# Cross-attention and expert layer: the router and the query sums moved behind two up blocks, the order at both ends rebuilt

## Chip, cores and metric

The kernel runs on one core of one Trainium2 chip. The metric is the device time of one execution, in microseconds (us). TensorE does the matrix products, VectorE is called DVE, ScalarE ACT, GpSimd POOL, SyncE SP.

## What is computed

There are 32 batches of 256 rows of width 256, a context of 77 rows for each batch, and a mask over these 77 rows. The layer normalization of the rows gives queries, keys and values; the context is normalized with learned vectors and gives further keys and values, so that each of the 256 queries sees 333 keys in 4 heads of 64. Queries and keys are normalized to unit mean square. Behind the attention stands a second layer normalization and a layer of experts: a router takes two of eight experts for each row, from the better of two groups, and a shared block is added.

```python
def attention(x, latents, mask):          # x: context, latents: normalized rows
    xn = layernorm(x, ln_x_g, ln_x_b); ln = layernorm(latents, ln_l_g, ln_l_b)
    q = ln @ W_q
    kv = concatenate([xn @ W_kv, ln @ W_kv], axis=1)
    sim = einsum('bhid,bhjd->bhij', rmsnorm(q, q_gamma) * SCALE, rmsnorm(k, k_gamma))
    attn = softmax(where(full_mask, sim, -max))
    return einsum('bhij,bhjd->bhid', attn, v) @ W_out + b_out
...
topk_idx, topk_w = _route(x, gate_weight, gate_bias)   # sigmoid, best group of 2, two experts
r2 = maximum(einsum('th,eih->tei', x, up_weights), 0) ** 2
routed = einsum('tei,ehi,te->th', r2, down_weights, cw)
sh = maximum(x @ shared_up_weight.T, 0.0)
shared = sh * sh @ shared_down_weight.T
...
x = x + attention(ctx, _layernorm(x), mask)
x = x + experts(_layernorm(x))
```

## The kernel before

Each 32-bit product is made of three: every operand is split into a rounded high part and the low part that is left, and `split_product` (lines 292 to 297) adds high by high, high by low and low by high. So beside each product stand small operations that make the low parts: `hid_lo`, `x_lo`, `q_lo`, `k_lo`, `at_lo`, `ln_lo`, and for the weights `w_lo`, `up_lo`, `down_lo`.

The batches run in a pipeline of steps. Step b does the attention of batch b, the experts of batch b - 1, and the first layer normalization and the projections of batch b + 1. The first step has no experts, the last no projections, and a tail behind it does the experts of the last batch. Each engine has a program of its own whose order is written out by hand in its `step` function (TensorE from line 520, ScalarE from 731, DVE from 1079, GpSimd from 1271); semaphores order the engines among each other, and an engine that waits holds back all that stands behind in its program.

TensorE's step begins with `transpose_k` (the keys, line 362). Then come `sum_q_squares` (line 349: 32 small products, 32 columns at a time, that sum the squares of each query) and `router` (line 465: 32 more of that kind). Then two of the six up blocks of the experts, two pairs of score blocks (lines 383 to 387), two up blocks, two pairs of score blocks, the shared down block, and then the transposes of the probabilities between the first down blocks and the last up blocks. The second half has the product with the values (line 411), the projections, the down blocks 2 to 7 and `transpose_x2` (line 452), which brings the twice normalized rows into place for the next router.

PSUM is shared out as four banks for attention (`attn_ps`), two for up (`up_ps`) and two for down (`down_ps`). The sums and the router's logits are written to `attn_ps`, the down blocks alternate between the two banks of `down_ps`, and DVE adds each of them to `acc` (`add`, line 1067), weighted with `route_w`.

DVE's step: `k_low`, the statistics of the next batch, four masked score blocks with their row maxima (`mask_scores`, line 906), `negate_max` (line 913, which needs the scales of the queries), the first eight levels of the routing (lines 996 to 1017), four more masked blocks, and then the rest of the routing between the adds of the experts. GpSimd's step: `q_scales`, the low parts of the hidden pairs 0 to 2 (`low`, line 1268), `rstd_first`, `residual` (`x_res`, line 1242), the low parts 3 and 4, `ln_low`, the low part 5 and the powers for the next batch. `q_scales`, `k_scales` and both `rstd` are powers with the exponent -1/2 (line 1223); the others are sums and differences of two tensors. Ahead of the steps DVE and ScalarE split the weights in parts; the low parts of the up weights (`up_parts`) stand in DVE's first step, those of the down weights in GpSimd's first step (line 1282).

## Time and profile before

| what | before |
|---|---|
| median of 3 runs | 1172.76 us (1172.66 to 1172.81) |
| the profiled execution | 1171.52 us |
| its span | 1169.7 us |
| busy TensorE | 1145.7 us, 98% of the span |
| busy DVE | 1006.4 us, 86% |
| busy ACT | 801.6 us, 69% |
| busy POOL | 555.2 us, 47% |

The span runs from the first to the last instruction of the profiled execution; the rest of its time lies around it. A row of an engine's instructions in order of time gives the start in us from the begin of the span, the length in us, the engine, the line of the kernel, the operation with its result and operands, and how many alike are grouped; in brackets stands the idle time before it, with what ended that. Where the bracket is missing, the engine had no idle time before the row. Lengths of TensorE's instructions overlap, so the distance from one start to the next is what counts. A clock of 1.00 is TensorE's full clock, 0.50 half of it.

### The profile page before, as it was taken

The numbers are of one execution on the slowest core, as the hardware profiler recorded it, in microseconds if no ns is written. First come the engines' busy times: TensorE is split into PE (matmuls) and PEld (weight loads), VectorE is DVE, ScalarE is ACT, GpSimd is POOL, SyncE is SP. The second block draws the span as 40 slices with busy tenths as digits, with TensorE's granted clock in tenths as the row PEclk, the third lists the DMA queues.
The fourth block names the chain that finished last, engine by engine and source line by source line (L and its number), as shares of the span: only waits on it lengthen the run. The fifth ranks groups of instructions, "written<-read, shape, count | busy, mean of one in ns | idle before, by whom it ended". The sixth has DMA issues, their size and how long they took to land. (4 is left out here: it accounts for less than half of the span.)

```text
span 1169.7 us, 32985 instructions
## 1 busy us (share of the span) xinstructions
PE 1145.7 (98%) x11772; PEld 1070.1 (91%) x11772; DVE 1006.4 (86%) x3500; ACT 801.6 (69%) x1900; POOL 555.2 (47%) x473
## 2 busy tenths in 40 slices
PE   7799999999999999999999999999999999999997
PEld 6699999999999999999999999999999999999997
DVE  6688988889888889888899888899888899888877
ACT  5577766677766768766778666678666677666673
POOL 5445444445444445454445454444454444454442
PEclk8899999999999999999999999999999999999999
DMA  5000000000000000000000000000000000000000
GB/s 173 13 14 23 23 22 12 14 23 23 23 12 22 14 23 22 23 11 23 14 22 23 23 11 22 13 23 23 22 11 22 14 23 22 23 10 15 10 11 19
DMA packets 28145, 26.06 MB, mean 22 GB/s; under 512 B 6544, under 2 KB 27440, under 8 KB 27984
## 3 DMA queue, kind: packets, MB, share of 16 engines
q1 hardware_dynamic: 27904, 23.83, 6.5%
q8 instruction: 95, 1.56, 0.6%
q14 instruction: 66, 0.54, 0.2%
q0 software_dynamic: 80, 0.14, 0.1%
HBM read 15.57 MB, written 8.39 MB: 20 GB/s over the span
## 5 line engine op out<-in xcount | busy, mean ns | idle before, releaser
L1268 POOL TENSOR_TENSOR hid_lo<-relu,hid_hi 128x512 fp32r<-128x512 f32 x192 | 248.3, 1293 | 246.6 <-DVE hid_hi L1052 166.2
L295 PE MATMUL down_ps<-down_hi,hid_hi 128*128 128x256 f32 x768 | 233.6, 304 | 1.7 <-ACT hid_hi L726 1.0
L1067 DVE SCALAR_TENSOR_TENSOR acc<-down_ps,route_w,acc 128x256 f32<-128x256 f32 x512 | 222.0, 475 | 8.9 <-PE down_ps L297 8.2
L295 PE MATMUL up_ps<-x_hi,up_hi 128*128 128x256 f32 x768 | 226.8, 295 | 0.0
L297 PE MATMUL down_ps<-down_hi,hid_lo 128*128 128x256 f32 x768 | 215.9, 281 | 0.0
L296 PE MATMUL down_ps<-down_lo,hid_hi 128*128 128x256 f32 x768 | 215.7, 281 | 0.0
L296 PE MATMUL up_ps<-x_lo,up_hi 128*128 128x256 f32 x768 | 214.3, 279 | 0.0
L297 PE MATMUL up_ps<-x_hi,up_lo 128*128 128x256 f32 x768 | 214.2, 279 | 0.0
L676 ACT ACTIVATE probs<-masked,neg_max,q_scale 128x333 f32<-128x333 f32 x256 | 168.1, 658 | 3.4 <-DVE neg_max L913 3.4
L721 ACT ACTIVATE relu_sb<-up_ps 128x512 f32<-128x512 f32 x192 | 113.6, 592 | 72.4 <-PE up_ps L297 69.1
L295 PEld LDWEIGHTS down_ps<-down_hi,hid_hi 128*128 128x128 f32 x768 | 144.4, 188 | 14.2 <-issue 12.9
L295 PEld LDWEIGHTS up_ps<-x_hi,up_hi 128*128 128x128 f32 x768 | 144.0, 188 | 7.3 <-ACT relu_sb L721 6.5
L296 PEld LDWEIGHTS down_ps<-down_lo,hid_hi 128*128 128x128 f32 x768 | 145.2, 189 | 0.0
L297 PEld LDWEIGHTS up_ps<-x_hi,up_lo 128*128 128x128 f32 x768 | 144.4, 188 | 0.0
L297 PEld LDWEIGHTS down_ps<-down_hi,hid_lo 128*128 128x128 f32 x768 | 144.4, 188 | 0.0
L296 PEld LDWEIGHTS up_ps<-x_lo,up_hi 128*128 128x128 f32 x768 | 144.2, 188 | 0.0
L1223 POOL TENSOR_TENSOR rstd<-var,minus_half 128x2 f32<-128x2 f32 (+1 forms) x64 | 49.9, 780 | 167.7 <-DVE var L961 165.7
L683 ACT ACTIVATE up_stage<-attn_ps 111x384 f32<-111x384 f32 x256 | 117.3, 485 | 16.9 <-PE attn_ps L397 16.9
L729 ACT ACTIVATE relu<-relu_sb 128x512 f32<-128x512 f32 x192 | 119.7, 624 | 3.0
L653 ACT ACTIVATE k_sq<-attn_ps 111x512 f32<-111x512 f32 x64 | 31.5, 492 | 125.6 <-PE attn_ps L297 125.6
L906 DVE CUSTOM_DVE_ANT_0 masked<-attn_ps,mask_row 128x333 f32<-128x333 f32 x256 | 114.0, 498 | 2.1 <-issue 2.1
L397 PE MATMUL attn_ps<-ident,probs 128*111 128x128 f32 x768 | 107.7, 277 | 7.0 <-DVE row_max L906 6.9
(145 smaller groups left out, 2851.1 us busy)
## 6 DMA issues: line engine op xcount, KB each, us to landing
out<-acc SPq DMA_DIRECT2D x31, 256.0 KB, 2.2
x_first<-in_x SPq DMA_DIRECT2D x16, 256.0 KB, 2.7
w_stage<-in_x SPq DMA_DIRECT2D x16, 256.0 KB, 2.8
up_stage<-in_up_t SPq DMA_DIRECT2D x1, 1536.0 KB, 6.8
down_stage<-in_down_t SPq DMA_DIRECT2D x1, 1536.0 KB, 8.5
c_first<-in_ctx SPq DMA_DIRECT2D x16, 77.0 KB
w_stage<-in_ctx SPq DMA_DIRECT2D x16, 77.0 KB
w_stage<-in_w_kv SPq DMA_DIRECT2D x1, 512.0 KB, 4.1
```

The source lines that it names most:

```text
L295: nc.tensor.matmul(out_ap, s_hi, m_hi, start=first, stop=False)
L296: nc.tensor.matmul(out_ap, s_hi, m_lo, start=False, stop=False)
L297: return nc.tensor.matmul(out_ap, s_lo, m_hi, start=False, stop=last)
L397: last = nc.tensor.transpose(attn_ps[0:KC, u % PT_RING, c * P:(c + 1) * P], probs[:, u, c * KC:(c + 1) * KC], ident[:])
L676: nc.scalar.activation(probs[:, u, :], masked[:, u, :], ACT.Exp, bias=neg_max[:, u:u + 1], scale=q_scale[:, u:u + 1], accum_out=row_sum[:, ...
L683: nc.scalar.activation(probs_t[:, u % PT_SB, :], attn_ps[0:KC, u % PT_RING, 0:CH * P], ACT.Copy).then_inc(pt_done, 1)
L721: nc.scalar.activation(relu_sb[:, p % 2, :], up_ps[:, (p + 1) % 2, :], ACT.Relu).then_inc(relu_done, 1)
L729: nc.scalar.activation(relu2[:, p % 2, :], relu_sb[:, p % 2, :], ACT.Square).then_inc(relu2_done, 1)
L906: nc.vector.tensor_tensor_reduce(masked[:, u, :], attn_ps[:, u % SCORE_RING, 0:KEYS], mask_row[:], 1.0, -MASKED, ALU.add, ALU.max, row_max ...
L1067: nc.vector.scalar_tensor_tensor(acc[:, t, :], down_ps[:, (e + 1) % 2, t * D:(t + 1) * D], route_w[:, t, e:e + 1], acc[:, t, :], ALU.mult, ...
L1223: nc.gpsimd.tensor_tensor(dst, src, minus_half[0:src.shape[0], 0:src.shape[1]], ALU.pow).then_inc(done, 1)
L1268: nc.gpsimd.tensor_tensor(hid_lo[:, p % HID_RING, :], relu2[:, p % 2, :], hid_hi[:, p % HID_RING, :], ALU.subtract).then_inc(hid_lo_done, 1)
```

## The change

In the steps, TensorE does the sums of the squares and the router behind the second up block, one behind the other, and right ahead of the first scores; their results go to the two banks of `down_ps` in place of two parts of `attn_ps`. ScalarE makes the squares of the queries behind the high part of x and the router's exponentials behind the hidden pair 0. DVE takes the norms of the queries behind `k_low`. GpSimd does the low part of hidden pair 0 ahead of the scales of the queries. `transpose_x2` goes ahead of down block 6 (down block 5 in the last step), and DVE splits its low part of x around the second part of `k_normalize`.

At the beginning, DVE makes the low part of the first layer normalization itself; the low parts of the down weights move from GpSimd to DVE, in four pieces in later gaps of the first step; two of the up parts, the normalization of batch 1 and one part of the projection weights go behind the second group of masked blocks. At the end, the router of the tail goes behind two up blocks, DVE normalizes before the add of expert 3, makes the low part of x before the add of expert 5, and takes the low part of hidden pair 1 from GpSimd.

The diff, cut: left out are a wait on a weight part, the split of `layer_norm1` in `stats_first` and `aggregate_first`, a wait of `pt_out` on parts of the up weights, and the new argument of `x2_low` that names its parts.

```diff
@@ -343,10 +343,12 @@
             pe.wait_ge(head_sel_done, 1)
+        elif b > 1:
+            pe.wait_ge(acc_done, (b - 1) * ACC)
                 for tile in COLUMN_TILES:
-                    last = nc.tensor.matmul(attn_ps[tile, 0, t * H + 2 * ft:t * H + 2 * ft + 2],
+                    last = nc.tensor.matmul(down_ps[tile, 0, t * H + 2 * ft:t * H + 2 * ft + 2],
@@ -369,13 +371,9 @@
         if pair == 0:
-            pe.wait_ge(q_norm_done, b + 1)
             pe.wait_ge(k_lo_done, (b + 1) * FT)
-        elif pair == 1:
-            if experts:
-                pe.wait_ge(exp_neg_done, b)
-        else:
+        elif pair > 1:
...
@@ -457,12 +455,14 @@
             pe.wait_ge(gate_in, DMA)
+        else:
+            pe.wait_ge(acc_done, b * ACC)
                 for tile in COLUMN_TILES:
-                    last = nc.tensor.matmul(attn_ps[tile, 3, t * E:(t + 1) * E],
+                    last = nc.tensor.matmul(down_ps[tile, 1, t * E:(t + 1) * E],
@@ -473,7 +473,7 @@
             pe.wait_ge(x2_hi_done, (b + 1) * FT)
-            pe.wait_ge(x2_lo_done, (b + 1) * FT)
+            pe.wait_ge(x2_lo_done, b * FT + 1)
@@ -481,6 +481,8 @@
                 cols = slice((2 * p + j) * P, (2 * p + j + 1) * P)
+                if p == 0 and j == 0 and k == 1:
+                    pe.wait_ge(x2_lo_done, (b + 1) * FT)
@@ -498,6 +500,8 @@
                 pe.wait_ge(acc_done, b * ACC)
+            if b + 1 < B:
+                pe.wait_ge(q_norm_done, b + 2)
@@ -510,8 +514,8 @@
             pe.wait_ge(acc_done, b * ACC + 2 * e - 1)
-        elif not first:
-            pe.wait_ge(acc_done, b * ACC - 2)
+        else:
+            pe.wait_ge(exp_neg_done, b + 1)
@@ -531,11 +535,11 @@
         transpose_k(b)
+        ffn("up", 0)
+        ffn("up", 1)
             router(f, f_first)
-        ffn("up", 0)
-        ffn("up", 1)
@@ -565,8 +569,8 @@
             ffn("down", 4)
+            transpose_x2(b)
             ffn("down", 5)
-            transpose_x2(b)
@@ -587,8 +591,8 @@
         project_q(b + 1)
+        transpose_x2(b)
         ffn("down", 6)
-        transpose_x2(b)
@@ -604,9 +608,9 @@
     steps(step)
-    router(B - 1, False)
     up(B - 1, 1, False, False)
+    router(B - 1, False)
@@ -643,6 +647,9 @@
         nc.scalar.activation(q_hi[:], qv, ACT.Copy).then_inc(q_hi_done, 1)
+    def q_square(b):
+        qv = up_ps[:, 0, :].rearrange("p (f s) -> p f s", f=FT)
...
@@ -712,7 +721,7 @@
             act.wait_ge(router_step, (b - 1) * ROUTER_STEPS + 1)
-        nc.scalar.activation(exp_neg[:], attn_ps[:, 3, 0:T * E].rearrange("p (t e) -> p t e", t=T),
+        nc.scalar.activation(exp_neg[:], down_ps[:, 1, 0:T * E].rearrange("p (t e) -> p t e", t=T),
@@ -733,9 +742,9 @@
         k_high(b, first)
+        ffn(0)
             router_exp(f, f_first)
-        ffn(0)
@@ -772,6 +781,8 @@
         x2_high(b, first)
+        if following:
+            q_square(b + 1)
@@ -788,11 +799,12 @@
     q_out(0, True)
+    q_square(0)
     steps(step)
+    hidden(B - 1, 0, False)
     router_exp(B - 1, False)
-    hidden(B - 1, 0, False)
...
@@ -849,6 +863,10 @@
             nc.vector.tensor_copy(ln_hi[:, ft, :], ln_t[:, ft, :]).then_inc(ln_hi_done, 1)
+            if first:
+                dve.wait_ge(ln_hi_done, ft + 1)
+                nc.vector.tensor_tensor(ln_lo[:, ft, :], ln_t[:, ft, :], ln_hi[:, ft, :],
+                                        ALU.subtract).then_inc(ln_lo_done, 1)
@@ -861,7 +879,7 @@
             dve.wait_ge(q_scale_done, b)
-        nc.vector.tensor_scalar(q_norm[:], attn_ps[:, 0, 0:U], DH * RMS_EPS * RMS_EPS, None,
+        nc.vector.tensor_scalar(q_norm[:], down_ps[:, 0, 0:U], DH * RMS_EPS * RMS_EPS, None,
...
@@ -1051,6 +1069,13 @@
+    def hidden_low_second(b):
+        dve.wait_ge(*hid_hi_ready(b, 1))
+        dve.wait_ge(relu2_done, b * PAIRS + 2)
+        dve.wait_ge(hid_lo_done, b * PAIRS + 1)
+        nc.vector.tensor_tensor(hid_lo[:, 1 % HID_RING, :], relu2[:, 1, :], hid_hi[:, 1 % HID_RING, :],
+                                ALU.subtract).then_inc(hid_lo_done, 1)
@@ -1076,6 +1101,13 @@
+    def down_parts(*parts):
+        for i in parts:
+            dve.wait_ge(w_hi_done, 4 + QUART + i)
+            rows = DOWN_ROWS[i]
+            nc.vector.tensor_tensor(down_lo[:, rows, :], down_stage[:, rows, :], down_hi[:, rows, :],
+                                    ALU.subtract).then_inc(down_lo_done, 1)
@@ -1094,8 +1126,9 @@
         k_low(b, 1)
+        q_norms(b, first)
         if first:
-            normalize1(1, False)
+            variance1(1, False)
@@ -1107,7 +1140,7 @@
         if first:
-            up_parts(1, 2, 3)
+            up_parts(1)
@@ -1116,6 +1149,11 @@
             mask_keys(b + 1)
+        if first:
+            up_parts(2, 3)
+            normalize1(1, False)
+            dve.wait_ge(w_hi_done, 3)
+            split_lo(w_lo[:, :, WOUT], w_stage[:, :, WOUT], w_hi[:, :, WOUT])
@@ -1138,38 +1176,44 @@
             add(2)
-            add(3)
             layer_norm2(b, first)
+            add(3)
+            normalize2(b, first)
             add(4)
-            normalize2(b, first)
+            x2_low(b)
             add(5)
-            x2_low(b)
         ln_high(b + 1, False)
+        if first:
+            down_parts(0, 1)
         add(5)
+        if first:
+            down_parts(2)
         k_norms(b + 1, 1, False)
+        if first:
+            down_parts(3)
         k_normalize(b + 1, 0, False)
+        x2_low(b, 0)
         k_normalize(b + 1, 1, False)
-        x2_low(b)
+        x2_low(b, 1)
         add(6)
-        q_norms(b + 1, False)
@@ -1190,20 +1234,18 @@
     k_norms(0, 0, True)
-    dve.wait_ge(w_hi_done, 3)
-    split_lo(w_lo[:, :, WOUT], w_stage[:, :, WOUT], w_hi[:, :, WOUT])
+    stats_first(1)
     k_norms(0, 1, True)
-    layer_norm1(1, False)
-    variance1(1, False)
     k_normalize(0, 0, True)
+    aggregate_first(1, False)
     q_low(0)
-    q_norms(0, True)
     route(f, *range(1, 10))
+    hidden_low_second(f)
@@ -1275,13 +1317,10 @@
+        low(0)
         if first:
-            for i, rows in enumerate(DOWN_ROWS):
-                pool.wait_ge(w_hi_done, 4 + QUART + i)
-                nc.gpsimd.tensor_tensor(down_lo[:, rows, :], down_stage[:, rows, :], down_hi[:, rows, :],
-                                        ALU.subtract).then_inc(down_lo_done, 1)
-        low(0)
+            rstd_first(1, False)
@@ -1313,14 +1352,15 @@
     rstd_first(0, True)
-    ln_low(0)
     k_scales(0, 1, True)
-    rstd_first(1, False)
     for p in range(PAIRS):
-        hidden_low(B - 1, p)
+        if p == 2:
+            pool.wait_ge(hid_lo_done, (B - 1) * PAIRS + 2)
+        if p != 1:
+            hidden_low(B - 1, p)
```

## Rows read from the trace of the kernel before

**Rows 1.** TensorE in order of time, one step: start us, us, line, operation, repeats.
```profile
513.28 0.75 PE L362 MATMUL attn_ps<-ident,k_rms 111*128 111x111 f32 x6
513.97 0.43 PE L349 MATMUL attn_ps<-head_sel,q_sq 128*32 128x2 f32 x32
514.24 0.44 PE L465 MATMUL attn_ps<-gate_stage,x_full 128*32 128x8 f32 x32
514.62 0.39 PE L295 MATMUL up_ps<-x_hi,up_hi 128*128 128x256 f32 x1
...
517.66 0.42 PE L383 MATMUL attn_ps<-k_hi,q_hi 64*128 64x334 f32 x2
...
534.74 0.37 PE L295 MATMUL down_ps<-down_hi,hid_hi 128*128 128x256 f32 x1
```

**Rows 2.** TensorE in order of time: first instruction of the second and last step.
```profile
54.30 1.12 PE L362 MATMUL attn_ps<-ident,k_rms 111*128 111x111 f32 x6 [0.92 <-DVE k_rms L886]
...
1113.04 0.75 PE L362 MATMUL attn_ps<-ident,k_rms 111*128 111x111 f32 x6
```

**Rows 3.** GpSimd in order of time, the same step; idle before in brackets.
```profile
515.87 1.64 POOL L1223 TENSOR_TENSOR q_scale<-q_norm,minus_half 128x8 f32<-128x8 f32 x1 [2.75 <-DVE q_norm L864]
518.26 1.30 POOL L1268 TENSOR_TENSOR hid_lo<-relu,hid_hi 128x512 fp32r<-128x512 f32 x1 [0.76 <-ACT relu L729]
519.94 1.30 POOL L1268 TENSOR_TENSOR hid_lo<-relu,hid_hi 128x512 fp32r<-128x512 f32 x1 [0.37 <-ACT relu L729]
522.42 1.32 POOL L1268 TENSOR_TENSOR hid_lo<-relu,hid_hi 128x512 fp32r<-128x512 f32 x1 [1.19 <-ACT relu L729]
523.70 0.85 POOL L1223 TENSOR_TENSOR rstd<-var,minus_half 128x3 f32<-128x3 f32 x1
524.52 1.29 POOL L1242 TENSOR_TENSOR x_res<-x_first,bout_row 128x512 f32<-128x512 f32 x1
```

**Rows 4.** DVE in order of time, the same step.
```profile
515.70 0.87 DVE L1067 SCALAR_TENSOR_TENSOR acc<-down_ps,route_w,acc 128x256 f32<-128x256 f32 x2
...
520.59 0.66 DVE L913 SCALAR_TENSOR_TENSOR neg_max<-row_max,q_scale 128x4 f32<-128x4 f32 x1
...
522.00 0.17 DVE L1003 TENSOR_TENSOR pair_hi<-biased 128x8 f32<-128x8 f32 x1
...
522.62 1.14 DVE L1010 TENSOR_TENSOR top<-mid_a,mid_b 128x4 f32<-128x4 f32 x1
523.79 0.16 DVE L1012 TENSOR_TENSOR group_sum<-top 128x4 f32<-128x4 f32 x1
...
524.15 0.50 DVE L906 CUSTOM_DVE_ANT_0 masked<-attn_ps,mask_row 128x333 f32<-128x333 f32 x1
...
533.57 0.86 DVE L1067 SCALAR_TENSOR_TENSOR acc<-down_ps,route_w,acc 128x256 f32<-128x256 f32 x2
```

**Rows 5.** GpSimd and DVE in order of time, the last step.
```profile
1123.43 1.29 POOL L1242 TENSOR_TENSOR x_res<-w_stage,bout_row 128x512 f32<-128x512 f32 x1
1123.52 1.21 DVE L1012 TENSOR_TENSOR group_sum<-top 128x4 f32<-128x4 f32 x1
```

**Rows 6.** Beginning, GpSimd and DVE; last row by windows: stretch, length, busy engines, clock.
```profile
10.46 1.26 POOL L1234 TENSOR_TENSOR ln_lo<-ln_t,ln_hi 128x333 fp32r<-128x333 f32 x1 [0.27 <-DVE ln_hi L851]
...
22.77 0.73 DVE L841 TENSOR_SCALAR x_hat<-w_stage,mv,rstd 128x256 f32<-128x256 f32 x2
...
23.74 0.95 DVE L1072 TENSOR_TENSOR up_lo<-up_stage,up_hi 128x768 fp32r<-128x768 f32 x1
...
26.44 1.73 DVE L913 SCALAR_TENSOR_TENSOR neg_max<-row_max,q_scale 128x4 f32<-128x4 f32 x1
28.09 5.91 DVE L1072 TENSOR_TENSOR up_lo<-up_stage,up_hi 128x768 fp32r<-128x768 f32 x3
...
22.97:40.03 17.06, 9.51 (x46) 7.96 (x47) 13.56 (x34) 9.23 (x24) 12.15 (x6) 0.50 0.08 21
```

**Rows 7.** TensorE in order of time, the end of the last step.
```profile
1144.26 0.44 PE L452 MATMUL attn_ps<-ident,x_hat 128*128 128x128 f32 x2 [2.32 <-DVE x_hat L968]
```

More of the change, by code:

```diff
@@ L436, in project_out @@
                 if b == 0 and t == 0:
-                    pe.wait_ge(w_lo_done, 3)
+                    pe.wait_ge(w_lo_done, 3 + QUART)
                 pe.wait_ge(at_hi_done, b * T + t + 1)
@@ L680, in pt_out @@
                 act.wait_ge(pt_ps, b * U + u + 1)
+                if first and u < QUART:
+                    act.wait_ge(w_lo_done, 2 + u + 1)
                 if not first:
@@ L807, in layer_norm1, with stats_first @@
             def layer_norm1(b, first):
-                k = b * LN1_STEPS
+                stats_first(b)
+                aggregate_first(b, first)
+            def stats_first(b):
                 dve.wait_ge(x_loaded[b % 2], (b // 2 + 1) * DMA)
@@ L816, in layer_norm1, with aggregate_first @@
                 nc.vector.bn_stats(stats1[0:C, T, :], c_in[b % 2]).then_inc(ln1_step, 1)
-                dve.wait_ge(ln1_step, k + T + 1)
+            def aggregate_first(b, first):
+                dve.wait_ge(ln1_step, b * LN1_STEPS + T + 1)
                 carry(CARRY1)
@@ L970, in normalize2, with x2_low @@
                 last.then_inc(x2_hat_done, 1)
-            def x2_low(b):
-                for ft in range(FT):
+            def x2_low(b, *parts):
+                for ft in parts or range(FT):
                     dve.wait_ge(x2_full_done, b * FT + ft + 1)
```

## Prediction

> **What bounds the kernel now.** I read the page first: the span of 1169.7 us, of which TensorE is busy 98%. Then TensorE's instructions in order of time for one steady step, from the first transpose of the keys (called T0, here 513.28) to the next [rows 1]: no row there has an idle figure behind it, and the steps from the second to the last-but-one repeat at (1113.04 - 54.30)/30 = 35.29 us [rows 2]. Before 54.30 lies the beginning, behind 1113.04 the last step and the tail, 1169.7 - 1113.04 = 56.66. So the kernel is 54.30 + 30 x 35.29 + 56.66, plus 1.82 outside the span (1171.52 - 1169.7).
>
> A step bound by TensorE says nothing of how much room the others have. That is seen in GpSimd's and DVE's instructions of the same step [rows 3, 4], and they are nearly a second bound: DVE's chain from the first row maxima to the accumulation of expert 2 ends at 534.43 (533.57 + 0.86), and expert 4's down block, which waits for it, starts at 534.74 [rows 1, 4]. The reader should look at DVE's durations: one of the two maxima called `top` takes 1.14 where the like `group_sum` takes 0.16. It began 0.20 after GpSimd's low part of hidden pair 2 (522.42) and ended just behind it (523.74). `neg_max` takes 0.66 and ends at 521.25, 0.01 behind pair 1's low part (519.94 + 1.30). So a DVE operation with two SBUF inputs that starts behind such a GpSimd operation is held until that one ends. `pair_hi`, before it, is not held. `group_sum` ran in 0.16 inside `rstd`, GpSimd's power [rows 3, 4]; power operations do not hold.
>
> The Trainium skill, page "SBUF — State Buffer", section Who interferes with whom, states that a DVE instruction with two SBUF inputs contends with a GpSimd instruction that reads SBUF, and that the second to issue fully blocks. For the subtractions the trace agrees (1.14 against 0.16); for the power, which reads SBUF too, it does not (0.16 inside 0.85). By the rule alone the step would be longer still: rival three.
>
> **The step, TensorE's side.** Sums (513.97 to 514.24, 0.27) and router (514.24 to 514.62, 0.38) leave the place behind the transposes and go behind the second up block, before the first scores. The first up block starts now 1.34 after T0. It may take the place of the sums, 0.69 after T0, less the change into their column tiles, which no row shows alone; I estimate 0.53, between 0.40 and 0.69. Router to up block costs 0.38 - 0.27 = 0.11 over the sums' own length [rows 1], and up to router comes anew, so four changes of tile shape become three. I take -0.17 per step, between -0.38 and -0.05. So the scores start 517.66 - 513.28 = 4.38 - 0.17 = 4.2 after T0, with all that follows.
>
> The Trainium skill, page "TensorEngine Tiling (Array Packing)", section Key Properties, says that changing the tiling mode drains TensorE; by it the new direct change from router to scores (32 columns at a time to 64 rows) is not free. The nearest row is the 0.11 above, and with it twice the gain of -0.17 would be about -0.06.
>
> **The step, GpSimd's and DVE's side.** In order:
> 1. Low part 0 goes before the query scales in GpSimd's queue. It comes 518.26 - 514.62 = 3.64 behind the first up block, so at 0.53 + 3.64 = 4.17 to 5.47. The query scales (1.64) now wait for it: 5.47 to 7.05. Low part 1 (1.30) follows at 7.0 and ends at 8.3, not 7.96 [rows 3]. The query norms come at about 4.3, in time.
> 2. `neg_max` for the first four blocks needs the scales and has two SBUF inputs. It starts inside low part 1 and is held to 8.3: +0.35.
> 3. Low part 2 starts with its up block, 522.42 - 513.28 = 9.14 - 0.17 = 8.97. `pair_hi`, 522.00 or 8.72 before, comes at 8.72 + 0.35 = 9.07. Before, it was 0.42 ahead of low part 2; now it is 0.10 behind, and is held to 10.28. If it slips through, its neighbour `pair_lo`, 0.08 later, is held.
> 4. Four operations that had been done before the hold now stand behind it. From `pair_hi` to the maximum that was held took 522.62 - 522.00 = 0.62, of which 0.17 is `pair_hi` itself, so 0.45 is left when it ends. `group_sum` and `group_sel` follow 0.20 apart each (two operations of 0.16 that wait for one another fill the 0.36 from `group_sum` to the fifth mask): 10.28 + 0.45 + 0.40 = 11.13 to 11.15.
> 5. `x_res` on GpSimd starts 524.52 - 523.74 = 0.78 behind low part 2 (after `rstd`): at 11.06, to 12.35. `group_sel` is 0.09 behind it. Such a thing is seen in the last step: `x_res` at 1123.43, `group_sum` at 1123.52, held for 1.21 [rows 5]. So `group_sel` ends at 12.36.
> 6. The masks of the fifth score block, 524.15 or 10.87 before, start at 12.37: +1.5. From there to the end of expert 2's accumulation DVE has no gap: 534.43 - 524.15 = 10.28. It ends at 22.65; expert 4's down block, 21.46 before (534.74), starts at about 22.7. The rest of the step, 35.29 - 21.46 = 13.83, is unchanged.
>
> Step: 22.71 + 13.83 = 36.54, +1.25. TensorE would wait for it mainly where the transposes of the first probabilities and the down blocks use DVE's row maxima and accumulator. Bounds: without item 5 the masks start at about 11.3 and the step is +0.15 to +0.25; with both holds at full length, +1.5; with none, -0.17. I take item 5, because its case has been seen at the same distance, 0.09 [rows 5].
>
> Three waits are new on TensorE. The sums wait for the last add of the batch before (515.70 + 0.87, 3.29 after T0 [rows 4]); with the scores at 4.2, less 0.27 and 0.38, they come at 3.55, so 0.26 is to spare, and behind them stand router, scores and all that follows, for nobody can pass. The shared block waits for the query norms and expert 0's block for the exponentials, both due four blocks earlier: nothing.
>
> The moves with one answer: `q_square` and `router_exp` on ScalarE go behind an operation on which the next stage waits, and leave the one that follows room; the query norms' place on DVE changes by 0.16 ahead of masks; the split waits on x's low part come earlier or at the same time. They hide in TensorE's up blocks (3.04 from the first to the scores). If that cover went, each would cost at most its own length of 0.2 to 0.4, taken into the range.
>
> **The beginning.** TensorE's first projection waits for GpSimd's low part of the layer norm, 10.46 + 1.26 = 11.72. On DVE, where the like 768-column part takes 0.95 when nothing holds it (23.74), it costs under half: start -1.2 (estimate: 1.26 less the 0.1 to 0.2 for its DVE time, and 0.1 of handover). On DVE, `neg_max` took 1.73 (0.66 in a steady step), held by the down weights' low parts on GpSimd: -1.1. The normalization of batch 1 (22.77, before the up part at 23.74: 0.97) goes behind the second masks. The three up parts in front of these masks (28.09, 5.91) become one of 0.95: -4.96 [rows 6]. Together -8.2; the scores and the probabilities come sooner only as TensorE and ScalarE do, of which I take off 0.3. What comes back: two up parts, the normalization and a weight part stand behind the masks, and four down parts on DVE in gaps: 0.3 to 0.9 late before the second step's transposes, and I take 0.6 and another 0.5 for a chain of ScalarE that is now the latest. So -6.8; the first transpose of the second step moves from 54.30 to 47.5, bounds -4.5 to -7.5. TensorE's granted clock was 0.50 from 22.97 to 40.03 and 1.00 behind that [rows 6]; where it stays at the half, the bound of -4.5 holds.
>
> **The end.** The last transposes of x wait 2.32 for the normalization [rows 7]; expert 3's accumulation (0.86, as expert 2's) stands between the layer norm's statistics and it and goes behind it: -0.6 to -0.85. But the last down block needs expert 5's sum, now behind the low part of x, which waits for ScalarE: about +1.2. The later route chain of that step adds 0.3, and the tail's low part on DVE is neutral. Sum +1.0 (-0.8 to +1.5): 56.66 becomes 57.7.
>
> **Sum.** 47.5 + 30 x 36.54 + 57.7 = 1201.4; with 1.82 outside 1203.2, against 1171.52 of the profiled execution: +31.7. The runs' median is 1172.76, so I predict **1204.5**. Its own range is 1197 to 1213 (begin and end, and 0.2 to 0.3 of a step either way).
>
> **Rivals.**
> - *TensorE stays the bound.* DVE's routing slips ahead of low part 2: decided where `top` and its two fellows start before that operation, which takes 0.16 or more less shift than items 2 and 3 give, and the fifth mask by about 11.2. Then 30 x -0.17 = -5.1, -6.8 and +1.0: -10.9, 1172.76 - 10.9 = 1162. For it: the shifts are differences of small numbers, and DVE had spare time before 534.74 of 0.3. Against: low part 1 is pushed behind 1.64 of scales, a plain sum.
> - *Only the first hold.* `group_sel` is done before `x_res` starts (0.1 earlier than item 5 has it). Step +0.15 to +0.2: 30 x 0.17 = +5.1, less 5.8: 1172, no change to speak of.
> - *The power holds too.* `rstd` then holds `pair_lo` to 11.1, `x_res` the next to 12.35, and the rest of the chain, 0.9, follows: masks at 13.3, step +2.2: 47.5 + 30 x 37.5 + 57.7 + 1.8 = 1232. Against it is `group_sum`'s 0.16 inside `rstd`, in every steady step. The Trainium skill's page "SBUF — State Buffer", section Who interferes with whom, gives this rival its rule.
>
> **How the numbers follow.** Forecast 0.63; TensorE-bound 0.18; only the first hold 0.16; the power 0.03. A time within 0.2%, about 2.3 us, is what a measurement here can't tell from no change. The second rival spreads over all three: 0.05 faster, 0.05 same, 0.06 slower. So faster 0.23, same 0.05, slower 0.72. The range reaches to the first rival: 1161 to 1213 leaves out half of that rival, the third one and the forecast's edges.
>
> **What would show it.** Right: low part 1 ends about 8.3 after T0, `pair_hi` or `pair_lo` takes about 1.2, `group_sel` about 1.2 inside `x_res`, the fifth mask starts 12.4 after T0, and TensorE has idle time behind DVE's `row_max` and accumulator in each step. Wrong: the fifth mask at 10.9 to 11.3, no idle TensorE, steps of 35.1; or `x_res` that starts later than 11.2, because `rstd` was late. Beginning and end are shown by the first transposes of the second and the last step.

## The result and the profile after

The changed kernel takes 1206.72 us (median of four runs, 1206.31 to 1207.74) against 1172.71 before: 1.0291 times as long, 95% interval 1.0273 to 1.0309. The profiled execution took 1206.73 with a span of 1205.0, 35.3 more than before. The prediction was 1204.5.

| stretch of the span | before | predicted | after |
|---|---|---|---|
| begin to the second step's first transpose | 54.30 | 47.5 | 46.30 |
| one of 30 steps | 35.29 | 36.54 | 36.64 |
| last step's first transpose to the end | 56.66 | 57.7 | 59.57 |

The step is (1145.43 - 46.30)/30, the end 1205.0 - 1145.43. TensorE in order of time, changed kernel: the first instruction of the second step, then the step whose first transpose (T0) is at 522.92, then the first of the last step.

```profile
46.30 0.60 PE L364 MATMUL attn_ps<-ident,k_rms 111*128 111x111 f32 x4 [0.99 <-DVE k_rms L904]
...
522.92 0.79 PE L364 MATMUL attn_ps<-ident,k_rms 111*128 111x111 f32 x6
523.48 0.36 PE L295 MATMUL up_ps<-x_hi,up_hi 128*128 128x256 f32 x1
...
526.48 0.43 PE L351 MATMUL down_ps<-head_sel,q_sq 128*32 128x2 f32 x32
526.76 0.44 PE L465 MATMUL down_ps<-gate_stage,x_full 128*32 128x8 f32 x32
527.18 0.42 PE L381 MATMUL attn_ps<-k_hi,q_hi 64*128 64x334 f32 x2
...
535.99 1.41 PE L395 MATMUL attn_ps<-ident,probs 128*111 128x128 f32 x9 [0.41 <-DVE row_max L924]
...
545.78 0.36 PE L295 MATMUL down_ps<-down_hi,hid_hi 128*128 128x256 f32 x1 [0.22 <-DVE acc L1092]
...
1145.43 0.79 PE L364 MATMUL attn_ps<-ident,k_rms 111*128 111x111 f32 x6
```

Read beside [rows 1]: the scores start 4.26 after T0 instead of 4.38, so TensorE's own side of the change is a gain. Expert 4's down block starts 545.78 - 522.92 = 22.86 after T0 instead of 21.46: 1.40 is lost, and 1.52 between scores and down block. The two brackets name who was late, DVE with its row maxima and with its accumulator. Read as distances from one start to the next, the first transposes of the probabilities come 0.57 later behind the shared down block than before, and expert 4's down block 0.47 later behind the transposes ahead of it; the other 0.5 lies among the instructions in between, without a bracket. A steady step of the kernel before had no such bracket.

GpSimd and DVE in the same step, the lines that answer to [rows 3] and [rows 4]:

```profile
527.10 1.30 POOL L1310 TENSOR_TENSOR hid_lo<-relu,hid_hi 128x512 fp32r<-128x512 f32 x1 [4.35 <-ACT relu L738]
528.36 1.64 POOL L1265 TENSOR_TENSOR q_scale<-q_norm,minus_half 128x8 f32<-128x8 f32 x1
529.96 1.30 POOL L1310 TENSOR_TENSOR hid_lo<-relu,hid_hi 128x512 fp32r<-128x512 f32 x1
531.95 1.29 POOL L1310 TENSOR_TENSOR hid_lo<-relu,hid_hi 128x512 fp32r<-128x512 f32 x1 [0.69 <-ACT relu L738]
533.20 0.86 POOL L1265 TENSOR_TENSOR rstd<-var,minus_half 128x3 f32<-128x3 f32 x1
534.03 1.29 POOL L1284 TENSOR_TENSOR x_res<-x_first,bout_row 128x512 f32<-128x512 f32 x1
```

```profile
530.24 1.03 DVE L931 SCALAR_TENSOR_TENSOR neg_max<-row_max,q_scale 128x4 f32<-128x4 f32 x1
...
532.02 1.25 DVE L1021 TENSOR_TENSOR pair_hi<-biased 128x8 f32<-128x8 f32 x1
...
533.72 0.16 DVE L1028 TENSOR_TENSOR top<-mid_a,mid_b 128x4 f32<-128x4 f32 x1
533.91 0.16 DVE L1030 TENSOR_TENSOR group_sum<-top 128x4 f32<-128x4 f32 x1
534.11 1.23 DVE L1033 TENSOR_TENSOR group_sel<-group_sum 128x2 f32<-128x2 f32 x1
535.26 0.15 DVE L1035 TENSOR_TENSOR group_sel<-group_sum 128x2 f32<-128x2 f32 x1
535.34 0.49 DVE L924 CUSTOM_DVE_ANT_0 masked<-attn_ps,mask_row 128x333 f32<-128x333 f32 x1
```

Each long DVE operation ends within 0.03 of a GpSimd subtraction or sum: `neg_max` at 531.27 (low part 1 at 531.26), `pair_hi` at 533.27 (low part 2 at 533.24), `group_sel` at 535.34 (`x_res` at 535.32). Before there were two such holds in this stretch, now there are three. The third begins 0.08 behind `x_res`. Inside `rstd`, the power, the second `top` and `group_sum` take their 0.16, as `group_sum` did before. The step shown is no exception: `pair_hi` and `group_sel` are held in 30 steps of this trace.

### The profile page after: what moved, and what is told of

Read it like the earlier page. It is cut to its first block and busy times, and to the rows that moved or that the text cites. A ratio compares the mean times of both kernels' runs of the same rounds, so it can differ in the third digit from the quotient of the medians.

```text
span 1205.0 us, 33050 instructions
## 1 busy us (share of the span) xinstructions
PE 1168.3 (97%) x11772; PEld 1077.1 (89%) x11772; DVE 1024.1 (85%) x3507; ACT 806.0 (67%) x1900; POOL 540.8 (45%) x466
## 5 line engine op out<-in xcount | busy, mean ns | idle before, releaser
L1092 DVE SCALAR_TENSOR_TENSOR acc<-down_ps,route_w,acc 128x256 f32<-128x256 f32 x512 | 216.9, 473 | 2.4 <-PE down_ps L297 1.8
L395 PE MATMUL attn_ps<-ident,probs 128*111 128x128 f32 x768 | 115.6, 284 | 13.1 <-DVE row_max L924 13.0
L395 PEld LDWEIGHTS attn_ps<-ident,probs 128*111 128x111 f32 x768 | 97.8, 178 | 23.3 <-issue 18.5
```

The lines of the kernel that those rows point to most:

```text
L395: last = nc.tensor.transpose(attn_ps[0:KC, u % PT_RING, c * P:(c + 1) * P], probs[:, u, c * KC:(c + 1) * KC], ident[:])
L1092: nc.vector.scalar_tensor_tensor(acc[:, t, :], down_ps[:, (e + 1) % 2, t * D:(t + 1) * D], route_w[:, t, e:e + 1], acc[:, t, :], ALU.mult, ...
```

## The experiments

Theory one is the prediction's: DVE is late because `x_res` runs when `group_sel` comes. Its rivals: the down blocks' PSUM banks, now shared by sums and router (theory two); the swap of the scales and low part 0 on GpSimd by itself (three); `x_res` costing DVE its length wherever it stands (four); more work on DVE (five).

**The residual a little later.** GpSimd's order stays; `x_res` waits until `group_sel` is written.

```diff
+                if experts:
+                    pool.wait_ge(router_step, (b - 1) * ROUTER_STEPS + 12)
                 residual(b, first)
```

> Edit to the changed kernel: in every step GpSimd's residual (x_res) waits until DVE's routing has written group_sel, and nothing else. Theory one (group_sel is held by x_res, item 5 of the prediction): group_sel takes 0.16 instead of 1.23, the fifth masked block starts about 11.35 after the step's first transpose instead of 12.42, the step falls from 36.62 to about 35.55, and the time to about 1174. Theory two (the step is long because the sums and the router use the down blocks' PSUM banks, so that TensorE and DVE wait for each other there): the step stays at 36.6 and the time at 1206.

Measured: 1173.73 us (ten runs), 1.0011 times the kernel before (1.0002 to 1.0021); 33.0 us of the changed kernel's time are gone. The step is 35.57 ((1113.11 - 46.05)/30). DVE, GpSimd and TensorE in the step with T0 508.78:

```profile
517.88 1.19 DVE L1021 TENSOR_TENSOR pair_hi<-biased 128x8 f32<-128x8 f32 x1
...
519.91 0.16 DVE L1033 TENSOR_TENSOR group_sel<-group_sum 128x2 f32<-128x2 f32 x1
520.07 0.50 DVE L924 CUSTOM_DVE_ANT_0 masked<-attn_ps,mask_row 128x333 f32<-128x333 f32 x1
```

```profile
520.22 1.29 POOL L1284 TENSOR_TENSOR x_res<-x_first,bout_row 128x512 f32<-128x512 f32 x1 [0.36 <-DVE group_sel L1035]
```

```profile
530.51 0.36 PE L295 MATMUL down_ps<-down_hi,hid_hi 128*128 128x256 f32 x1 [0.20 <-DVE acc L1092]
```

A wait of 0.36 on GpSimd takes 1.07 off the step. `group_sel` is back at 0.16; the fifth mask starts 11.29 after T0 instead of 12.42; `x_res` now runs beside masks, which read PSUM and one SBUF operand and keep their 0.50. Theory two falls: sums and router still use the down blocks' banks here. What is left of the lateness, the one bracket on TensorE, would be that of the holds behind low parts 1 and 2, which this run leaves; the run with the masks first shows it.

**The scales first.** The two lines of GpSimd's program change places back.

```diff
-                low(0)
                 q_scales(b, first)
+                low(0)
```

> Edit to the changed kernel: GpSimd makes the scales of the queries ahead of low part 0 again. Theory one: the query norms come only 4.07 after the step's first transpose, so low part 1 ends at about 8.5 all the same, neg_max is held to there, pair_hi still starts inside low part 2 and ends with it; what stands behind is unchanged, the step 36.6 to 36.7 and the time 1206 to 1209. Theory three (the swap of the two on GpSimd made DVE late): the step falls to 35.3 to 35.6 and the time to 1167 to 1176.

Measured: 1210.58 us (one run), steps of 36.81 ((1150.35 - 46.07)/30). Theory three falls, for putting the order back brings nothing back. The step is 0.17 longer than that of the changed kernel and 0.1 above the range expected, the time 1.6 above it. The rows of DVE (T0 524.55) show why:

```profile
531.88 1.16 DVE L931 SCALAR_TENSOR_TENSOR neg_max<-row_max,q_scale 128x4 f32<-128x4 f32 x1
...
533.58 1.28 DVE L1018 TENSOR_TENSOR biased<-score,gbias 128x16 f32<-128x16 f32 x1
534.89 0.17 DVE L1021 TENSOR_TENSOR pair_hi<-biased 128x8 f32<-128x8 f32 x1
...
535.71 1.20 DVE L1030 TENSOR_TENSOR group_sum<-top 128x4 f32<-128x4 f32 x1
536.94 0.16 DVE L1033 TENSOR_TENSOR group_sel<-group_sum 128x2 f32<-128x2 f32 x1
```

DVE reaches low part 2 one operation earlier in its list, at `biased`, so one more operation has to be done after the hold, and `x_res` catches `group_sum` instead of `group_sel`. It is so in 27 steps; in four others `pair_hi` and `group_sel` are held, as in the changed kernel. The end of a hold is fixed by GpSimd; what it costs is what of DVE's list is still ahead when it ends.

**The residual first.** `x_res` goes to the begin of GpSimd's step, behind a wait on the low part of x, into time in which GpSimd was idle.

```diff
+                if experts:
+                    pool.wait_ge(x2_lo_done, b * FT)
+                residual(b, first)
                 low(0)
                 q_scales(b, first)
...
                     rstd_first(b + 1, False)
-                residual(b, first)
                 low(3)
```

> Edit to the changed kernel: GpSimd makes x_res at the begin of its step, behind the low part of x and ahead of low part 0, where it has been idle for over 4 us. Theory one (what costs the time is only that x_res runs when group_sel comes): as with the residual that waits for group_sel, group_sel takes 0.16, the fifth masked block starts at 11.3, the step is 35.5 to 35.6 and the time 1172 to 1174. Theory four (x_res costs DVE its 1.2 wherever it stands, as some two-input operation is held): the step stays at 36.4 to 36.6 and the time at 1200 to 1206.

Measured: 1173.62 us (ten runs), 1.0007 times the kernel before (0.9997 to 1.0016); steps of 35.58 ((1113.48 - 46.06)/30). It is the time of the later residual, from the other side, and theory four falls: here `x_res` meets DVE operations that read an operand from PSUM, none of the routing's is held by it, and it costs nothing.

**The masks first.** Added to the residual first: DVE masks blocks five to eight behind the routing's third level, and does the levels from the fourth on when GpSimd has finished.

```diff
-                routing(1, 2, 3, 4, 5, 6, 7, 8)
+                routing(1, 2, 3)
                 mask_scores(b, 4, first)
...
-                routing(9, 10, 11, 12)
+                routing(4, 5, 6, 7, 8, 9, 10, 11, 12)
```

> Edit to the changed kernel: x_res at the begin of GpSimd's step as in the run before, and DVE masks the blocks five to eight right behind the first three levels of the routing; the other levels come behind these masks, when GpSimd is idle. Theory one (DVE's two holds behind low parts 1 and 2 are all that is left of its lateness, and without the second TensorE is the bound again): no small routing operation takes over 0.3 in a steady step, TensorE has no idle time, the step is 35.10 to 35.20 and the time 1160 to 1163. Theory five (DVE is late for other reasons, its own work grew): the step stays at 35.4 to 35.6, 1170 to 1174.

Measured: 1160.28 us (1159.92 to 1161.55), 0.989 times the kernel before (0.9876 to 0.9905), faster than the kernel before and than the residual first. Steps of 35.15 ((1101.32 - 46.94)/30). DVE with T0 504.32:

```profile
511.64 1.04 DVE L931 SCALAR_TENSOR_TENSOR neg_max<-row_max,q_scale 128x4 f32<-128x4 f32 x1
...
513.55 0.50 DVE L924 CUSTOM_DVE_ANT_0 masked<-attn_ps,mask_row 128x333 f32<-128x333 f32 x1 [0.15 <-issue]
...
515.57 0.16 DVE L1021 TENSOR_TENSOR pair_hi<-biased 128x8 f32<-128x8 f32 x1
...
516.57 0.17 DVE L1033 TENSOR_TENSOR group_sel<-group_sum 128x2 f32<-128x2 f32 x1
```

The fifth mask starts 9.23 after T0, the routing runs without a hold, and no TensorE instruction from 504.32 to 539.50 has idle time before it. Only `neg_max` is still held (1.04); with TensorE the bound, that costs nothing. Theory five falls: DVE does the same work here. What was left of theory two falls too: the sums and the router use the same banks.

**The same with the last step of before.** In the last step TensorE's transposes of x stand behind down block 5 again, and DVE's adds of experts 3 and 5 go back to their places.

```diff
                     ffn("down", 4)
-                    transpose_x2(b)
                     ffn("down", 5)
+                    transpose_x2(b)
                     ffn("down", 6)
```

> Edit to the changed kernel: as the run with the masks first, and the last step in the order of the kernel before (transposes of x behind down block 5, expert 3 added before the layer norm, expert 5 before the low part of x). Theory one: steps of 35.10 to 35.20, an end 0.5 shorter than with the changed order where the clock does the same in both; time 1159 to 1163. Rival (the order of the end is worth nothing): the same time as the run with the masks first within 0.3.

Measured: 1161.21 us (1159.66 to 1161.64), no difference from its fellow that the runs can tell. In the profiles the end is 1159.0 - 1101.12 = 57.9 against 1159.8 - 1101.32 = 58.5, with the clock at half for 3.41 us in both: the 0.5 that was expected.

**The last step of before, on the changed kernel.** The same edit, alone; DVE's side of it is this.

```diff
                     add(2)
+                    add(3)
                     residual_half(b, 0)
                     residual_half(b, 1)
                     layer_norm2(b, first)
-                    add(3)
-                    normalize2(b, first)
                     add(4)
-                    x2_low(b)
+                    normalize2(b, first)
                     add(5)
+                    x2_low(b)
```

> Edit to the changed kernel: in the last step TensorE's transposes of x stand behind down block 5 again, and DVE adds expert 3 before the layer norm and expert 5 before the low part of x. Theory one (the end is 2.86 longer because down block 5 no longer fills the time before the transposes' wait and TensorE's clock then falls for it): the stretch from the last step's first transpose to the end falls from 59.5 to about 57.4, the clock does not fall between them and the tail's up blocks, and the time is about 1204.6. Rival (the end is longer because the router of the tail stands between up blocks and the masks are late): it stays at 59 to 59.5 and the time at 1206 to 1206.7.

Measured: 1207.03 us (1206.21 to 1207.28), no gain. The end is 1205.5 - 1146.52 = 58.98 against 59.57: 0.6 of the 2.1 expected, so the rival was the nearer one. TensorE's clock fell in it all the same, and that part of the expectation was wrong; more on it stands with the reasons below.

**The beginning alone.** The kernel before with only its beginning rebuilt: `ln_lo` and the down weights' low parts on DVE, two up parts, the normalization of batch 1 and a weight part behind the second masks.

```diff
                 if first:
-                    normalize1(1, False)
+                    variance1(1, False)
                     up_parts(0)
...
-                    up_parts(1, 2, 3)
+                    up_parts(1)
...
+                if first:
+                    up_parts(2, 3)
+                    normalize1(1, False)
+                    split_lo(w_lo[:, :, WOUT], ...)
```

> Edit to the kernel before: only the beginning is rebuilt (low part of the first layer normalization and of the down weights on DVE, two up parts, the normalization of batch 1 and a weight part behind the second masks); steps and end are those of before. Theory one (the beginning's gain is its own): the second step's first transpose comes at 46.3 to 47.0 instead of 54.30, steps are 35.28, and the time is 1164.7 to 1165.7. Rival (what the beginning gains hangs on the new places of sums and router): it comes at 50 or later and the time is 1168 to 1173.

Measured: 1164.89 us (1164.42 to 1166.13), 0.9939 times the kernel before (0.9924 to 0.9954). The second step begins at 46.14, and the steps are those of before, 35.29 ((1104.95 - 46.14)/30). The beginning's gain is its own.

**The beginning with residual and masks first, sums and router in their old places.** To the edit of the beginning come those of the residual and of the masks, the former ahead of the scales, which are the first of GpSimd's step there.

```diff
+                residual(b, first)
                 q_scales(b, first)
```

> Edit to the kernel before: the beginning rebuilt, x_res at the begin of GpSimd's step and the masks five to eight ahead of the levels four to eight of the routing; sums and router stay behind the transposes of the keys. It shows what the joined visit alone is worth when DVE is not late. Theory one (three changes of tile shape instead of four, 0.12 to 0.18 per step): this one has steps of 35.28, bound by TensorE, and about 1165, 4 to 5 more than its fellow with the joined visit. Rival (the joined visit is worth nothing to TensorE): both have the same step within 0.05.

Measured: 1164.71 us (1164.0 to 1165.4), 0.9926 times (0.9911 to 0.9941); steps of 35.28 ((1105.67 - 47.29)/30). As TensorE was the bound already, giving DVE room changes nothing: 1164.71 beside 1164.89 of the beginning alone. Its fellow with the joined visit needs 35.15 per step and 1160.28. So the joined visit is worth 0.13 per step when DVE is not late, 3.9 over the 30 steps; the two medians are 4.4 apart. The two kernels also differ in the other moves of the change within the step and at the end, so the 0.13 is that of all moves in a step. Most of it stands there by the scores: they start 4.38 after T0 in [rows 1], and 508.60 - 504.32 = 4.28 with the masks first.

## Why the prediction was right

**The step.** It went by its items, and each can be read in the rows after. Relative to T0: the first up block was foreseen at 0.53 and is at 0.56; the scores at 4.2 and 4.26; low part 0 at 4.17 and 4.18; the scales at 5.47 and 5.44; the end of low part 1 at 8.3 and 8.34; low part 2 at 8.97 and 9.03; `pair_hi` at 9.07 and 9.10, held to 10.28 and 10.35; `x_res` at 11.06 and 11.11; `group_sel` at 11.15 and 11.19; the fifth mask at 12.37 and 12.42; expert 4's down block at 22.7 and 22.86. Forecast +1.25, measured +1.35. Expert 4's down block is the one a little short: 0.16 late where the rest were 0.07 at most. The runs show that `group_sel` behind `x_res`, item 5, is the deciding one: with `x_res` out of its way, by a later or an earlier place, 1.07 of the 1.35 goes.

The margins were thin, as the prediction's chances said. `group_sel` came 0.08 behind `x_res`. How thin a margin may be, all ten traces together show: 313 of the routing's operations with two SBUF inputs took over 0.3, each of them began 0.010 or more behind a GpSimd subtraction or sum, and none that began ahead of one was held; one that began 0.020 behind still ran free. So 0.08 was enough. The rival "only the first hold" was this kernel with `x_res` 0.33 later (534.03 - 522.92 = 11.11 against 520.22 - 508.78 = 11.44): 1173.73 where the prediction gave that rival 1172. The rival "TensorE stays the bound" gave 1162, and the kernel in which DVE's routing meets no subtraction takes 1160.28. The third rival, the power that holds too, is out: `top` and `group_sum` ran in 0.16 inside `rstd`, at 533.72 and 533.91. The rule of the Trainium skill's page "SBUF — State Buffer", section Who interferes with whom, holds here for subtractions and sums, behind which DVE operations of 0.15 to 0.18 took up to 1.31, and not for a power that begins first: 966 of the routing's operations with two SBUF inputs began inside one in the ten traces, and none took over 0.17.

The price of the joined visit on TensorE, taken as -0.17 with bounds -0.38 and -0.05, is -0.13 with nobody late (35.28 to 35.15). The change from router to scores, which no row of before showed: 526.76 to 527.18 is 0.42 for the router's 32 products and the change, against 0.38 to an up block in [rows 1]. The Trainium skill's page "TensorEngine Tiling (Array Packing)", section Key Properties, has the mode change drain TensorE; no run here takes such a drain apart from the 0.42, and the gain that it would have brought down to 0.06 came out at 0.13.

**The beginning.** Foreseen -6.8, measured -8.0, outside its bounds of -4.5 to -7.5. The terms were about right and the giving back too large. TensorE and DVE at the beginning of the changed kernel:

```profile
10.75 0.46 PE L295 MATMUL attn_ps<-w_hi,ln_hi 128*111 128x512 f32 x1 [0.34 <-DVE ln_lo L868]
```

```profile
24.30 0.16 DVE L931 SCALAR_TENSOR_TENSOR neg_max<-row_max,q_scale 128x4 f32<-128x4 f32 x1
24.38 0.95 DVE L1097 TENSOR_TENSOR up_lo<-up_stage,up_hi 128x768 fp32r<-128x768 f32 x1
25.25 0.50 DVE L924 CUSTOM_DVE_ANT_0 masked<-attn_ps,mask_row 128x333 f32<-128x333 f32 x1
...
34.82 2.51 DVE L1108 TENSOR_TENSOR down_lo<-down_stage,down_hi 128x768 fp32r<-128x768 f32 x2
```

Beside [rows 6]: the first projection waited for a low part that ended at 11.72 and now starts at 10.75; `neg_max` takes 0.16 instead of 1.73; the second masks, which stood behind 28.09 + 5.91 = 34.0, start at 25.25. That is -8.7, and 0.7 of it comes back until the second step, where the prediction took off 1.4. The step of it that failed in size is the last one, the chain of ScalarE and the moved parts, which cost half of what was taken off. That ScalarE's chain is the latest was foreseen rightly. In the nine traces with the new beginning, the second step begins 21.66 to 21.73 behind ScalarE's first row of probabilities, and that row starts between 24.37 and 25.64. In the changed kernel it stood behind the high parts of the down weights, and these behind a transfer, which landed later still in the run with only the last step of before. ScalarE there, first the changed kernel:

```profile
21.68 3.05 ACT L629 ACTIVATE down_hi<-down_stage 128x768 fp32r<-128x768 f32 x4 [0.95 <-DMA down_stage<-in_down_t]
```

and then the run with only the last step of before, whose second step begins at 47.37:

```profile
22.68 3.04 ACT L629 ACTIVATE down_hi<-down_stage 128x768 fp32r<-128x768 f32 x4 [2.17 <-DMA down_stage<-in_down_t]
```

**The end.** Foreseen +1.0 (-0.8 to +1.5), measured 59.57 - 56.66 = +2.9, outside its bounds. Two things are in it, the change and a fall of TensorE's clock. The granted clock by stretches (stretch, length, busy time of TensorE, its weight loads, DVE, ACT and POOL, then the clock, 1.00 being the level of 2.4 GHz and 0.50 that of 1.2), around TensorE's wait for the transposes of x and behind it. The first row is of the changed kernel:

```profile
1177.45:1180.86 3.41, 3.09 (x15) 2.82 (x14) 2.42 (x6) 0.75 (x3) 0.00 (x0) 0.50 0.00 0
```

The second is of the kernel with only the beginning rebuilt, whose end is that of before word for word:

```profile
1135.89:1139.30 3.41, 2.87 (x14) 2.87 (x15) 2.47 (x8) 1.21 (x4) 0.00 (x0) 0.50 0.00 0
```

The third is the same stretch of the kernel before:

```profile
1143.73:1147.14 3.41, 2.88 (x52) 2.72 (x53) 2.73 (x8) 1.40 (x5) 0.00 (x0) 1.00 0.01 2
```

In the third row the stretch holds the router's 32 small products and 20 other matmuls, in the second 14.

The end can be taken in two at the start of these transposes, the row that [rows 7] shows for the kernel before. Here it is of the changed kernel:

```profile
1176.47 0.44 PE L450 MATMUL attn_ps<-ident,x_hat 128*128 128x128 f32 x2 [2.45 <-DVE x_hat L986]
```

of the kernel with only the beginning rebuilt:

```profile
1136.43 0.69 PE L452 MATMUL attn_ps<-ident,x_hat 128*128 128x128 f32 x2 [2.56 <-DVE x_hat L976]
```

and of the run with the later residual:

```profile
1143.14 0.44 PE L450 MATMUL attn_ps<-ident,x_hat 128*128 128x128 f32 x2 [2.45 <-DVE x_hat L986]
```

The last column says whether the clock fell for 3.41 us near this row, and each line is one execution.

| kernel | last step's first transpose to the transposes of x | from there to the end | sum | fall of 3.41 |
|---|---|---|---|---|
| before | 31.22 | 25.44 | 56.66 | no |
| beginning alone | 31.48 | 26.77 | 58.25 | yes |
| last step of before, on the changed kernel | 31.85 | 27.13 | 58.98 | yes |
| changed | 31.04 | 28.53 | 59.57 | yes |
| residual a little later | 30.03 | 27.96 | 57.99 | no |

From each of the first four lines to the next, one thing changes in the end. The fall alone, with the program of before, costs 1.59. The changed step and tail, with the last step's old order, cost 0.73 more: 0.37 ahead of the transposes, where the prediction had 0.3 for the later route chain, and 0.36 behind them, where it called the tail neutral. The new order of the last step gives -0.81 (foreseen -0.6 to -0.85) and +1.40 (foreseen +1.2). That is the 2.9. With a fall on both sides the change is worth 59.57 - 58.25 = 1.32, within the bounds; the prediction's own terms add up to 0.65 to 0.9, not to 1.0. The steps that failed are the clock, which it priced only at the beginning, and the tail, which it put at nothing.

Without a fall the changed end would not be that near. The run with the later residual has none, but it also lacks a hold that the changed kernel has in its last step, of `top` behind `x_res`:

```profile
1155.69 1.30 POOL L1284 TENSOR_TENSOR x_res<-w_stage,bout_row 128x512 f32<-128x512 f32 x1
1155.79 1.22 DVE L1024 TENSOR_TENSOR top<-pair_hi 128x4 f32<-128x4 f32 x1
```

By it the fifth mask starts 12.31 after the step's first transpose, and 11.24 in the run with the later residual; it is the 1.01 between 31.04 and 30.03. Behind the transposes the fall costs 28.53 - 27.96 = 0.57 in the new order, and 26.77 - 25.44 = 1.33 in that of before. In the new order TensorE waits for DVE's accumulator before the last down block, 1.10 at the full clock and 0.32 with the fall, so the half clock fills a wait. An estimate from these rows for the changed end without a fall is 57.99 + 1.01 = 59.0, which is 2.3 above the end before and outside the bounds too.

So the total was nearer than its parts: the beginning 1.2 better than foreseen, thirty steps 2.9 worse, the end 1.9 worse, 3.6 together in the span. The runs' time stands only 2.2 above the forecast, for the changed kernel's median lies 1.7 above the profiled span where the forecast added 3.1. That these partly cancel is luck; the range would have held without it.

## What to carry to other kernels

Lay the GpSimd sums and subtractions over DVE's two-input operations, as intervals relative to the step's begin, before an order is changed: a move that frees 0.13 of the bounding engine can push one tiny operation 0.08 behind the start of a GpSimd operation of 1.3 and lose eight times as much (1.07). The cure is as cheap as the harm: move the GpSimd operation into a time when DVE works on PSUM, or put DVE's PSUM work there, as the masks that kept their 0.50. A change of order that looks bad as a whole may hold two good parts, and it pays to time them apart, as the beginning alone (1164.89 against 1172.65, 0.994) and the joined visit with a free DVE (1160.28 against 1164.71, 0.996) did here.

## What the runs showed of the hardware that was not expected

A power on GpSimd does not hold DVE, but it can be held by it. At the beginning of the changed kernel a DVE operation with two SBUF inputs starts 0.10 ahead of the scales of the queries, and these take 2.34 instead of the 1.64 of a step:

```profile
21.60 0.94 DVE L1097 TENSOR_TENSOR up_lo<-up_stage,up_hi 128x768 fp32r<-128x768 f32 x1
21.70 2.34 POOL L1265 TENSOR_TENSOR q_scale<-q_norm,minus_half 128x8 f32<-128x8 f32 x1 [3.54 <-DVE q_norm L882]
```

One SBUF input instead of two does not make a DVE operation safe. In the tail of the changed kernel `sig_den`, which reads one, begins 0.11 behind a low part and takes 1.22, where it took 0.16 in the last step:

```profile
1184.53 1.29 POOL L1310 TENSOR_TENSOR hid_lo<-relu,hid_hi 128x512 fp32r<-128x512 f32 x1 [8.89 <-ACT relu L738]
1184.64 1.22 DVE L1014 TENSOR_SCALAR sig_den<-exp_neg 128x16 f32<-128x16 f32 x1 [2.57 <-ACT exp_neg L724]
```

How much of the tail's 0.36 that is, no run shows.

The half clock in the rebuilt beginning was not on the path. It lasted 17.06 us in the kernel before and 6.83 in the run with the masks first; in that run with the old end the clock stayed at the full level through this stretch. Rows by stretches of these last two; the masks first:

```profile
22.99:29.82 6.83, 6.17 (x34) 5.01 (x31) 6.76 (x28) 6.00 (x16) 2.62 (x2) 0.50 0.01 2
```

and then the same with the old end:

```profile
22.97:40.03 17.06, 12.20 (x112) 9.27 (x109) 14.40 (x43) 12.48 (x33) 5.10 (x4) 1.00 0.02 6
```

Their second steps begin at 46.94 and 46.96, 21.71 and 21.70 behind ScalarE's first row of probabilities. In the end a fall of 3.41 costs 1.6 with the order of before. It stands in six of the ten traces, and the program does not decide it: the run with the beginning alone has it and the kernel before has not, and with the new order of the end the run with the masks first has it and the one with the residual first has not. Why is open.
